# Key fills of two context chunks at once (500 columns), context splits one step sooner, and loads of row sums placed later, in a gated cross-attention and expert kernel

## The reference

```python
def xattn(query, key, value):                       # key = value = ctx_1024
    q = (query @ Wq.T).reshape(B, L, H, D) * D ** -0.5
    k = (key @ Wk.T).reshape(B, -1, H, D)
    v = (value @ Wv.T).reshape(B, -1, H, D)
    scores = jax.nn.sigmoid(jnp.einsum('blhd,bshd->bhls', q, k))
    return jnp.einsum('bhls,bshd->blhd', scores, v).reshape(B, L, E) @ Wo.T

x = x + jnp.tanh(g_xattn[0]) * xattn(_layernorm(x), ctx_1024, ctx_1024)
tokens = _layernorm(x).reshape(E, T, D)
h = gelu(jnp.einsum('etd,edf->etf', tokens, w1) + b1[:, None, :])
y = jnp.einsum('etf,efd->etd', h, w2) + b2[:, None, :]
x = x + jnp.tanh(g_ffn[0]) * y.reshape(x.shape)
```

## Time and profile before

| | before |
|---|---|
| Median of 3 runs | 1693.45 us (1690.64 to 1695.2) |
| The profiled execution | 1685.1 us |
| Its span, first to last instruction | 1683.4 us |
| TensorE busy | 1667.0 us, 99% |
| ScalarE busy | 787.1 us, 47% |
| VectorE busy | 753.4 us, 45% |
| TensorE's granted clock | 1.000 (2.4 GHz) |

### The profile page before, as it was taken

The page is one execution under the profiler, slowest core; times in us unless marked ns, Lnnn a source line. Parts: engine busy times, 40 slices in busy tenths (PEclk is TensorE's granted clock), DMA queues, the critical chain, the costliest instruction groups (busy, mean ns, idle before and its releaser), DMA issues.

```text
span 1683.4 us, 32954 instructions
## 1 busy us (share of the span) xinstructions
PE 1667.0 (99%) x12763; PEld 1509.8 (90%) x12763; DVE 753.4 (45%) x1290; ACT 787.1 (47%) x956; POOL 219.4 (13%) x323
## 2 busy tenths in 40 slices
PE   8999999999999999999999999999999999999999
PEld 7898898898898898898898888899999999999998
DVE  6343433433433334334334234464646465555554
ACT  5655555555555555555555455333333333334332
POOL 2122122122122122122122121000000000000000
PEclk9999999999999999999999999999999999999999
DMA  7887677686686776777677785446253543526251
GB/s 253 225 227 202 193 224 201 187 237 190 188 238 183 201 228 189 201 221 196 195 221 198 199 227 157 158 135 204 103 184 124 177 141 134 179 97 203 103 169 55
DMA packets 197686, 309.19 MB, mean 184 GB/s; under 512 B 28081, under 2 KB 155601, under 8 KB 197553
## 3 DMA queue, kind: packets, MB, share of 16 engines
q1 hardware_dynamic: 173632, 229.43, 48.4%
q0 software_dynamic: 23920, 77.95, 13.1%
HBM read 228.44 MB, written 78.84 MB: 183 GB/s over the span
## 4 chain that ended last, share of the span: by engine, by line
PE 96%; DVE 2%; DMA 1%; ACT 1%; issue 0%; SPq 0%; ACTq 0%; DVEq 0%; POOLq 0%
PE fill_ps L620 41%; PE scores_ps L798 18%; PE fill_ps L780 13%; PE scores_ps L652 10%; PE heads_ps L669 9%; PE heads_ps L780 4%; ACT probs L837 0%; DMA probs<-WKT_in 0%; PE scores_ps L620 0%; DMA part_scr<-part 0%; DMA k_st<-k_scr 0%; DMA v_sb<-w_in 0%; DVE wV L1187 0%; DVE wQ L1011 0%; DVE wK L1187 0%
## 5 line engine op out<-in xcount | busy, mean ns | idle before, releaser
L837 ACT ACTIVATE probs<-scores_ps 125x1792 f32<-125x1792 f32 x192 | 320.4, 1669 | 139.2 <-PE scores_ps L652 111.0
L798 PE MATMUL scores_ps<-ctx_hl,wK 128*128 128x448 f32 x1536 | 316.6, 362 | 0.0
L798 PEld LDWEIGHTS scores_ps<-ctx_hl,wK 128*128 128x128 f32 x1536 | 288.1, 188 | 19.8
L620 PE MATMUL fill_ps<-ctx_hl,wK 128*128 128x250 f32 x2304 | 298.2, 281 | 1.0 <-DVE wK L1011 0.6
L620 PEld LDWEIGHTS fill_ps<-ctx_hl,wK 128*128 128x128 f32 x2304 | 279.9, 189 | 7.8 <-issue 6.1
L620 PE MATMUL fill_ps<-wV,ctx_hl 128*125 128x512 f32 x1152 | 280.8, 394 | 0.0
L620 PEld LDWEIGHTS fill_ps<-wV,ctx_hl 128*125 128x125 f32 x1152 | 207.8, 185 | 46.3 <-DVE q_stage L1118 0.2
L780 PE MATMUL fill_ps<-wQ,wV 128*128 128x448 f32 x1152 | 243.6, 366 | 3.0 <-DVE wV L1187 3.0
L780 PEld LDWEIGHTS fill_ps<-wQ,wV 128*128 128x128 f32 x1152 | 215.8, 188 | 20.9 <-DVE wV L1187 3.7
L566 POOL DMA_DIRECT2D k_scr<-k_stage x192 | 139.4, 726 | 665.7 <-DVE k_stage L1115 509.3
L652 PEld LDWEIGHTS scores_ps<-q_st,k_st 96*125 96x125 f32 x1536 | 189.1, 188 | 19.4 <-issue 7.7
(11 more groups left out here) (98 smaller groups left out, 1347.5 us busy)
## 6 DMA issues: line engine op xcount, KB each, us to landing
k_st<-k_scr SPq DMA_DIRECT2D x576, 125.0 KB, 3.4
v_sb<-w_in SPq DMA_DIRECT2D x94, 512.0 KB, 4.5
k_scr<-k_stage POOLq DMA_DIRECT2D x192, 250.0 KB, 3.9
ctx_raw<-ctxT_in SPq DMA_DIRECT2D x48, 500.0 KB, 4.6
q_st<-q_scr SPq DMA_DIRECT2D x192, 112.0 KB, 3.3
probs<-w_in SPq DMA_DIRECT2D x32, 512.0 KB, 3.8
q_scr<-q_stage POOLq DMA_DIRECT2D x64, 224.0 KB, 4.2
x_res<-xT_in SPq DMA_DIRECT2D x16, 448.0 KB, 4.8
```

The source lines that it names most:

```text
L620: last = pe.matmul(out_, lhsT(kt, a), rhs(kt, c), start=(kt == 0 and t == 0), stop=(kt == KT - 1 and t == 2))
L798: last = pe.matmul(y_ps[:, dt, 0:T], w2[:, slot, a, k, dt * P:(dt + 1) * P], hid_hl[:, slot, d, k, :], start=(c == 0 and k == 0 and t == 0 ...
L837: nc.scalar.activation(probs[0:ST, s % VISIT], scores_ps[0:ST, :, 0:2 * L], ACT.Sigmoid, scale=SCALE).then_inc(s_probs, 1)
```

## The change

1. **Pairs of chunks.** Key fills with i % 3 == 0 outside b = -1 (`is_pair`) compute chunks 0 and 1 of a row block in one bank: 12 matmuls of 500 columns in the place of two fills of 12 matmuls of 250. Chunk 2 keeps its fill of 250. What leaves (ScalarE, VectorE) and the store (GpSimd's queue) are one instruction each for a pair; gathers stay as they are, one for each step. A batch has 8 key fills and no longer 12; b = -1 keeps its single ones.
2. **Order of the fills.** The lists are written anew: pairs at steps 1, 4, 7 and 9, and value 0 of the next batch stands ahead of the keys of chunk 2 in step 8.
3. **Context** splits move from steps 5, 6, 7 to 4, 5, 6, and the load of chunk 2 from step 6 to step 5.
4. **Sums.** `load_sums(-1)` moves from step 10 of b = -1 to step 0 of b = 0, behind the gathers there. In b = 0, `load_residual` moves from step 7 to 9. In expert 0, `load_sums(B)` moves from chunk 2 to chunk 4, and `moments(B)` from chunk 3 to chunk 5.
5. **Squares** of the folds of b = -1 and 0 lie in `x1T` (which is `x_res`) and no longer in `q_stage`. ScalarE's waits for stored queries and for the fold, ahead of a query's copy, fall away there; the load of the residual of b = 0 waits for the fold.

```diff
-    FILL = [(1, "K", 0), (1, "O", 0), (2, "K", 1), (2, "O", 1), (3, "K", 2), (3, "V", 2),
-            (4, "K", 3), (4, "V", 3), (5, "V", 4), (5, "V", 5), (6, "K", 4), (7, "K", 5), (7, "K", 6), (7, "Q", 0),
-            (8, "K", 7), (8, "V", 0), (9, "K", 8), (9, "K", 9), (9, "Q", 1), (10, "K", 10), (10, "V", 1),
-            (11, "K", 11), (11, "Q", 2), (11, "Q", 3)]
+    FILL = [(1, "K", 0), (1, "O", 0), (2, "O", 1), (3, "K", 2), (3, "V", 2), (4, "K", 3), (4, "V", 3), (5, "V", 4),
+            (5, "V", 5), (6, "K", 5), (7, "K", 6), (7, "Q", 0), (8, "V", 0), (8, "K", 8), (9, "K", 9), (9, "Q", 1),
+            (10, "V", 1), (11, "K", 11), (11, "Q", 2), (11, "Q", 3)]
...
-    CTX_SPLITS = {5: 0, 6: 1, 7: 2}
+    CTX_SPLITS = {4: 0, 5: 1, 6: 2}
...
+    def is_pair(b, i):
+        return b > -1 and i % 3 == 0
...
+            return x_t if known(b, B) else x1T if b < 1 else q_flat
...
-                    if s == {-1: 10, 0: 8}.get(b, 7) and not known(b, B):
+                    if known(b, 0) and s == 0:
+                        load_sums(-1)
+                    if s == (8 if known(b, 0) else 7) and attends(b):
                         load_sums(b)
-                    if s == (11 if known(b, B - 1) else 7) and attends(b):
+                    if s == {0: 9, B - 1: 11}.get(b, 7) and attends(b):
                         load_residual(b)
...
-                    if known(e, 0) and c == 2:
+                    if known(e, 0) and c == 4:
                         load_sums(B)
...
+                at(pool, s_k_in[(j + 1 - RING) % 3], 16 * COPIES * (4 * n + (j + 1 - RING) // 3 + 1))
                 own(pool)
-                pool.dma_start(scr["k"][j % RING].rearrange("h p s -> p h s"), k_stage[:, j % 3].bitcast(F32)
-                               ).then_inc(s_k_st[j % RING], 16)
+                pool.dma_start(scr["k"][j % RING:j % RING + 2].rearrange("r h p s -> p (r h) s"),
+                               k_stage[:, 0:2].rearrange("p r h s -> p (r h) s").bitcast(F32)
+                               ).then_inc(s_k_st[ring_sem(n, j)], 16)
...
+                    if is_pair(b, i):
+                        last = three_terms(ps[:, 0:2 * SC], lambda kt, a: w["K"][:, a, kt, mt * P:(mt + 1) * P],
+                                           lambda kt, a: ctx_hl[:, 0:2, a, kt, :])
...
+                        nc.scalar.copy(k_stage[:, 0:2, HI, :], ps[:, 0:2 * SC].rearrange("p (r s) -> p r s", s=SC)
+                                       ).then_inc(hi["K"], 1)
...
-                    if first and c == 3:
+                    if first and c == 5:
                         moments(B)
```

More of the change, by code:

```diff
@@ L81, in flamingo_block @@
     BANK_0 = {(k, i): g % 3 for g, (_, k, i) in enumerate(FILL_0)}
-    BANK_BESIDE = {(k, i): g % 3 for g, (_, k, i) in enumerate(FILL_LAST)} | {("K", 4): 2, ("K", 5): 2}
+    BANK_BESIDE = {(k, i): g % 3 for g, (_, k, i) in enumerate(FILL_LAST)} | {("K", 5): 2}
     BANK_LAST = {("O", 0): 0, ("O", 1): 1}
@@ L138, in tile_of, with keys_done, ring_sem @@
         return i % KT if kind == "Q" else i % 6 if kind == "V" else i
+    def is_pair(b, i):
+        return b > -1 and i % 3 == 0
+    def keys_done(n, j):
+        return K_FILLS * n + 2 + j + 1 - (j + 2) // 3
+    def ring_sem(n, j):
+        return j % RING if n == 0 and j < AHEAD else j % RING - (j % 3 == 1)
     def step_of(i):
@@ L354, in gather_k @@
                 r = j % 3
-                alone(sp, s_k_st[j % RING], 16 * (2 * n + j // RING + 1))
+                alone(sp, s_k_st[ring_sem(n, j)], 16 * (2 * n + j // RING + 1))
                 alone(sp, s_scores, STEPS * n + j - 2)
@@ L417, in load_residual @@
                 alone(sp, s_x1T_st, 16 * b)
-                if b > 0:
-                    alone(sp, s_fold, FOLD_STEPS * nth_fold(b, 1))
+                alone(sp, s_fold, FOLD_STEPS * nth_fold(b, 1 if b > 0 else 0))
                 sp.dma_start(x_res[:], io["xT"][b]).then_inc(s_xr_in, 16)
@@ L564, in store_k @@
                 at(pool, s_k_in[(j - RING) % 3], 16 * COPIES * (4 * n + (j - RING) // 3 + 1))
+                if not is_pair(b, i):
+                    own(pool)
+                    pool.dma_start(scr["k"][j % RING].rearrange("h p s -> p h s"), k_stage[:, j % 3].bitcast(F32)
+                                   ).then_inc(s_k_st[ring_sem(n, j)], 16)
+                    return
+                at(pool, s_k_in[(j + 1 - RING) % 3], 16 * COPIES * (4 * n + (j + 1 - RING) // 3 + 1))
                 own(pool)
-                pool.dma_start(scr["k"][j % RING].rearrange("h p s -> p h s"), k_stage[:, j % 3].bitcast(F32)
-                               ).then_inc(s_k_st[j % RING], 16)
+                pool.dma_start(scr["k"][j % RING:j % RING + 2].rearrange("r h p s -> p (r h) s"),
+                               k_stage[:, 0:2].rearrange("p r h s -> p (r h) s").bitcast(F32)
+                               ).then_inc(s_k_st[ring_sem(n, j)], 16)
             def body(b, h, par):
@@ L819, in ctx_hi @@
                 act.wait_ge(s_ctx_in[chunk_place(par, c)], 16 * (chunk_round(h, par, c) + 1))
-                at(act, full["K"], STEPS * (n - 1) + 9 + c + 1)
+                if n > 0:
+                    act.wait_ge(full["K"], keys_done(n - 1, STEPS - 3 + c))
                 at(act, full["V"], 6 * (n - 1) + 2 * (c + 1))
@@ L859, in leave @@
                     j = step_of(i)
-                    at(act, s_k_st[(j - 3) % RING], 16 * (2 * n + (j - 3) // RING + 1))
-                    nc.scalar.copy(k_stage[:, j % 3, HI, :], ps[:, 0:SC]).then_inc(hi["K"], 1)
+                    last = 2 * n + (j - 3) // RING + 1
+                    if last > 0:
+                        m, k = (n, j - 3) if j > 2 else (n - 1, j - 3 + STEPS)
+                        act.wait_ge(s_k_st[ring_sem(m, k)], 16 * last)
+                        if is_pair(b, i) and ring_sem(m, k + 1) != ring_sem(m, k):
+                            act.wait_ge(s_k_st[ring_sem(m, k + 1)], 16 * last)
+                    if is_pair(b, i):
+                        nc.scalar.copy(k_stage[:, 0:2, HI, :], ps[:, 0:2 * SC].rearrange("p (r s) -> p r s", s=SC)
+                                       ).then_inc(hi["K"], 1)
+                    else:
+                        nc.scalar.copy(k_stage[:, j % 3, HI, :], ps[:, 0:SC]).then_inc(hi["K"], 1)
                 elif kind == "Q":
@@ L864, in leave @@
                     at(act, s_q_st[(mt - 2) % KT], 16 * (n + mt // 2))
-                    if i == (2 if known(b, -1) else 0) and whiches(b):
+                    if i == 0 and b > 0 and whiches(b):
                         act.wait_ge(s_fold, FOLD_STEPS * nth_fold(b, whiches(b)[-1]))
@@ L878, in square @@
                     act.wait_ge(s_ew_lo[1], 1)
-                elif known(b, -1):
-                    for mt in range(2):
-                        act.wait_ge(s_q_st[mt], 16)
-                else:
+                elif b > 0:
                     for mt in range(KT):
@@ L958, in e_hi @@
                 if known(e, 0) and c == 0:
-                    act.wait_ge(full["V"] if m == 1 else full["K"], (6 if m == 1 else 12) * B)
+                    act.wait_ge(full["V"] if m == 1 else full["K"], 6 * B if m == 1 else keys_done(B - 1, STEPS - 1))
                 if m == 1:
@@ L1195, in split_hidden @@
                 if known(e, 0) and c == 0:
-                    dve.wait_ge(full["K"], 12 * B)
+                    dve.wait_ge(full["K"], keys_done(B - 1, STEPS - 1))
                     dve.wait_ge(full["V"], 6 * B)
```

33 lines of the change are left out of this document (19 added, 14 removed).

## The result

The changed kernel took **1674.35 us** (median of 5 runs, 1673.76 to 1679.78), the kernel before, run five times, 1690.64 us (1685.37 to 1695.2): a ratio of 0.9907, interval 0.9884 to 0.993, so 0.9% faster. The forecast was 1682.3 us, from 1677 to 1689. The two profiled executions, however, differ by only 5.3 us: 1685.1 (span 1683.4) before, 1679.78 (span 1678.1) after. Three differences for one change (16 us between medians, 5.3 between profiles, 11.1 in the forecast) are what the experiments had to explain.

What follows compares the result with a forecast made beforehand. TensorE was taken as the bound, busy 1667.0 of 1683.4 us at full clock. Pairs (-6.2), four removed waits (-2.93, -0.40, -0.37, -1.84) and a new one (+0.6) gave -11.1 us: 1693.45 to 1682.3 us, range 1677 to 1689.

Steps and rivals of the forecast that it cites:

- Pairs: Key fills on TensorE: 62 pairs of 500-column matmuls at 224.4 ns, 2.71 us a pair, gain 0.10 each, 6.2 us.
- What leaves: Copy, subtraction and store of a pair: about 0.58 us on ScalarE, 0.7 on VectorE, no wait, nothing gained or lost.
- rival 3: ScalarE held by a pair's late store (step 7 before step 9): slower, 1709 us at a 12 us landing; chance 0.06.
- The start: Scores of step 1, body 0: gathers go out earlier, so the whole 2.93 us wait for keys goes.
- The new wait: Scores of step 6, body 0: TensorE waits 0.6 us for probabilities, between 0 and 1.5.
- Step 8 and the last batch: Body 0's 0.40 us wait for a key bank and the last batch's 0.37 for probabilities both go.
- The first expert: Expert 0: w1 of chunk 3 is issued 8.6 us earlier, so TensorE's 1.84 us wait for it goes.
- The sum: All terms for the profiled execution: -6.2 - 2.93 - 0.40 - 0.37 - 1.84 + 0.6 = -11.1 us.
- The step that failed: Profiled execution to median of runs: the 8.35 us difference taken as it is, 1693.45 - 11.1 = 1682.3 us.
- Rival 1: Pairs save next to nothing (231.7 ns a matmul); only the waits go, 5.5 us: 1688.0 us; chance 0.14.
- rival 2: The start's wait only moves, through late key stores or slowed sums; some 3 us come back: 1685 us; chance 0.14.
- rival 4: An overlooked wait of 0.5 us in each batch, 15 x 0.5, eats most of the gain: 1690 us; chance 0.06.

Runs made afterwards that it cites:

- The halves: The changed kernel, but each pair is filled by two runs of 12 matmuls of 250 columns into one bank: 1679.46 us, 0.994 of the kernel before.

## Where the prediction was right, and where it failed

Compared at full clock and in the same group (spans 1683.4 and 1672.8), the change brings 10.6 us; the forecast of the mechanism was 11.1. By its steps:

- **Pairs.** Right, and smaller. The matmul takes 229 ns; taken were 224.4, and the line through 448 and 512 columns gave 225.8, so the two lines that bounded the sum were both too low; only the ceiling of 231.7 held. A usual batch has gone from 64.47 to 64.19 us, 0.07 a pair where 0.10 was forecast: 4.3 us in the place of 6.2. The halves show that it is the width. The Trainium skill (TensorE: Matmul & The Clock Gate, section "Back-to-back issue gap"), by which two merged matmuls save 2.5 ns, would have given 1.9 us as an estimate. The measured 4.3 lies between.
- **What leaves.** Right. ScalarE copies a pair in 0.58 us, VectorE subtracts it in 0.68, GpSimd's queue issues the store in 0.77. The DMA issues on the changed kernel's page, and the landing of the pairs' stores:

```profile
k_scr<-k_stage POOLq DMA_DIRECT2D x62, 500.0 KB, 4.7
...
k_scr<-k_stage POOLq DMA_DIRECT2D x68, 250.0 KB, 4.2
```

```profile
DMA to landing us min/median/max: 3.8/4.7/9.3
```

  ScalarE's waits on the changed kernel's trace (us in total, times, longest us):

```profile
ACT k_stage L893 <- PE fill_ps L641: 51.6, 61, 2.4
```

  The longest landing, 9.3 us, is past the 7.9 from which I had ScalarE stand still, but it belongs to the pair of step 1 of body 1 (issued at 103.91), and the next pair is copied 13 us later. The margin of rival 3 is about the pair of step 7, and those stores landed in 4.6 to 5.3 us in every body. ScalarE's copies of pairs (line 893) waited for TensorE only, never for a store. So the margin was not touched.
- **The start.** Right. The gathers went out at 29.29 (forecast near 30), the scores began at 38.66 (38.9). From the value fill to the scores it is 41.83 - 35.87 = 5.96 us before and 38.66 - 35.79 = 2.87 after: 3.1 us, 0.2 more than the bracket.
- **The new wait.** Right: 0.44 us of idle time, 0.6 by starts, at 61.64.
- **Step 8 and the last batch.** Right: 0.66 and 0.45 us by the lengths of those two batches, with the pairs' share taken off.
- **The first expert.** Right: 2.1 us by starts for a bracket of 1.84. `moments` in chunk 5 costs no wait.
- **The sum:** -4.3 - 3.1 - 0.66 - 0.45 - 2.1 + 0.6 = -10.0 of the 10.6; 0.6 stays open. That it comes so near the forecast of 11.1 is in part luck: the pairs brought 1.9 us less than forecast, and the waits 0.8 more.

**The step that failed** is the last one, from the profiled execution to the median: "The median of the runs stands 8.35 us above the profiled execution, and I take the difference as it is", with what it rests on, "its clock is granted in full in every slice". The difference of 8.35 us is no constant beside the change. Two things in it moved.

The first is a cost that the sum put at nothing: its term of 2.93 for the start's wait is the idle time alone, and in most executions the clock falls behind it. Of the 8.35 us 3.2 are that (1688.31 against 1685.1), and they went with the waits. The experiments bear the size out: with the start's load back the lower group is 5.6 us above the changed kernel's (1679.95 against 1674.35), 3.1 of them the wait; with all the sums' moves undone 3.3 us are left beside the waits. Most of the cost is at the start; how much the expert's wait adds is not told apart.

The second is the group, about 5 us. Two of the three runs shown stood above 1693 us, while four of the five of the changed kernel fell in the lower group. So 1693.45 - 1674.35 = 19.1 is 5.1 of the draw between groups (1693.45 - 1688.31), 3.2 of the clock, and 10.8 of the change as it was argued. Either of the two alone would have left the time within the range (1682.3 - 3.2 = 1679.1, 1682.3 - 5.1 = 1677.2); the 3 us that the range allows for the scatter of medians did not cover both. How far the draw goes is shown by the medians of the changed kernel in three sets of runs: 1674.35, 1677.2 and 1679.47 us, of which the last two lie within the range; that the first is the lowest of them is chance. Why one execution has these matmuls at 202.5 ns and the next at 206.7 is open. All variants show the two groups, so the edits are not their cause; whether they shift the share of the groups can't be told from these numbers.

None of the rivals came true. Rival 1 was right in part, on the size of the pair's gain; rival 2 came half true where the sums were moved without the pairs, and rival 4 only where the splits were moved back.

## What to carry to other kernels

Read more than the profiled execution: its clock and its distance to the median say whether a wait has a second price, and a wait in an otherwise full TensorE can cost nearly as much again behind it (here 1.5 to 2.9 us behind waits of 1.8 to 3.4). When two pieces of work are merged, their inputs must be ready together: bring the inputs forward in the same edit, or the merge costs more than it gives (here some 46 us, against the 4.3 that the pairs bring). And ask what stands in a queue behind a DMA that waits: each of the two long waits of this kernel went when a small load of row sums was moved behind other loads.
